# A transformer layer in float32: a second numerator buffer, the low planes' place and SyncE's order at steps 5 to 7

## What is computed

```
out = x + attention(xn) + ffn(xn)
attention: 16 heads of 16; Q, K, V = xn @ W.T + b; rotary embedding on Q and K;
           softmax(causal(Q K^T / 4)) V; concat @ Wo.T + bo
ffn:       h = relu(xn @ W_fc.T)^2;  y = h @ W_proj.T;
           5 steps of mem = 0.9 mem + y - [mem > 1], counting mem > 1; count / 5
```

## Time and profile before

| what | value |
|---|---|
| median of 3 runs | 2417.91 us (2417.7 to 2423.07) |
| the profiled execution | 2427.82 us |
| its span, first to last instruction | 2423.4 us |
| mean granted clock of TensorE | 0.965 |
| PE (TensorE matmul) busy | 2211.7 us, 91% |
| DVE (VectorE) busy | 1423.0 us, 59% |
| ACT (ScalarE) busy | 1436.5 us, 59% |
| POOL (GpSimd) busy | 1105.9 us, 46% |
| DMA | 297.45 MB, 123 GB/s |

### The profile page before, as it was taken

The page is one execution under the profiler, slowest core; times in us unless marked ns, Lnnn a source line. Parts: engine busy times, 40 slices in busy tenths (PEclk is TensorE's granted clock), DMA queues, the critical chain, the costliest instruction groups (busy, mean ns, idle before and its releaser), DMA issues.

```text
span 2423.4 us, 48395 instructions
## 1 busy us (share of the span) xinstructions
PE 2211.7 (91%) x16260; PEld 1410.4 (58%) x16260; DVE 1423.0 (59%) x2108; ACT 1436.5 (59%) x1669; POOL 1105.9 (46%) x1065
## 2 busy tenths in 40 slices
PE   3789999999998999999998999999999999999975
PEld 2656656566565656656565665656656565665632
DVE  5646665665656656565665656567565665666421
ACT  2175756656566565656656565566656656665662
POOL 2445454453544545354453545445354454544420
PEclk8899999999999999999999999999999999999987
DMA  3243453534545254453534445353454534444432
GB/s 126 93 126 107 118 160 87 166 94 117 150 108 163 83 142 130 114 166 87 161 96 125 141 117 156 84 170 110 116 151 101 163 88 136 136 123 142 106 97 55
DMA packets 167726, 297.45 MB, mean 123 GB/s; under 512 B 25009, under 2 KB 112817, under 8 KB 155057
## 3 DMA queue, kind: packets, MB, share of 16 engines
q1 hardware_dynamic: 167472, 294.01, 42.6%
HBM read 173.32 MB, written 102.76 MB: 114 GB/s over the span
## 4 chain that ended last, share of the span: by engine, by line
PE 62%; DVE 10%; issue 8%; DMA 7%; SPq 6%; ACT 5%; POOL 2%; DVEq 0%; ACTq 0%; POOLq 0%
PE pair L984 23%; PE pair L1171 14%; PE pair L1135 13%; PE pair L1154 10%; DMA qk_dram<-rot 6%; ACT probs L640 3%; SPq L343 3%; DVE rot L775 3%; SPq L388 1%; DVE count L857 1%; SPq L334 1%; DVE stats L722 1%; DVE rot L768 1%; PE pair L996 1%; POOL probs L553 1%
## 5 line engine op out<-in xcount | busy, mean ns | idle before, releaser
L640 ACT ACTIVATE probs<-pair 128x1024 f32<-128x1024 f32 x1152 | 1115.3, 1026 | 588.1 <-PE pair L1154 587.8
L1171 PE MATMUL pair<-probs,v_sb 128*17 128x512 f32 (+3 forms) x6144 | 584.9, 514 | 78.0 <-DVE numer L880 63.5
L553 POOL TENSOR_SCALAR_AFFINE_SELECT probs<-probs 128x512 f32<-128x512 f32 x512 | 396.0, 793 | 527.6 <-ACT probs L640 527.6
L545 POOL TENSOR_TENSOR h_lo<-h_sq,h_hi 128x512 fp32r<-128x512 f32 x256 | 385.4, 1506 | 469.7 <-DVE h_hi L843 469.2
L1154 PE MATMUL pair<-q_ring,k_ring 64*128 64x512 f32 (+3 forms) x3072 | 450.6, 386 | 48.7 <-ACT probs L640 26.1
L1154 PEld LDWEIGHTS pair<-q_ring,k_ring 64*128 64x128 f32 x3072 | 229.6, 187 | 328.2 <-ACT probs L640 170.3
L841 DVE TENSOR_TENSOR h_sq<-h_sq 128x512 f32<-128x512 f32 x256 | 189.0, 738 | 330.5 <-ACT h_sq L631 328.7
L1171 PEld LDWEIGHTS pair<-probs,v_sb 128*17 128x17 f32 x6144 | 155.0, 99 | 389.3 <-issue 282.6
L1135 PE MATMUL pair<-wproj_hi,h_hi 128*128 128x256 f32 x1024 | 293.3, 286 | 5.1 <-POOL h_lo L545 5.0
L631 ACT ACTIVATE h_sq<-pair 128x512 f32<-128x512 f32 x256 | 153.2, 598 | 238.7 <-PE pair L984 189.3
L857 DVE SCALAR_TENSOR_TENSOR count<-y_sb,count 128x512 bf16<-128x512 f32 x256 | 290.4, 1134 | 6.7
(11 more groups left out here) (87 smaller groups left out, 2587.9 us busy)
## 6 DMA issues: line engine op xcount, KB each, us to landing
q_ring<-qk_dram SPq DMA_DIRECT2D x384, 128.0 KB
k_ring<-qk_dram SPq DMA_DIRECT2D x384, 128.0 KB
qk_dram<-planes SPq DMA_DIRECT2D x64, 512.0 KB, 2.9
qk_dram<-rot SPq DMA_DIRECT2D x64, 512.0 KB, 3.7
xn<-in_x SPq DMA_DIRECT2D x16, 1024.0 KB, 8.5
rs<-in_x SPq DMA_DIRECT2D x64, 256.0 KB, 2.9
acc_dram<-rs SPq DMA_DIRECT2D x64, 256.0 KB, 4.4
attn<-numer SPq DMA_DIRECT2D x256, 64.0 KB, 2.3
```

The lines of the kernel that those rows point to most:

```text
L545: pool.tensor_tensor(h_lo[i % HB][:, :], h_sq[i % HB][:, :], h_hi[i % HB][:, :].bitcast(F32), ALU.subtract).then_inc(h_lo_done, 1)
L553: ins = pool.affine_select(view, view, [[0, 4], [1, P]], ALU.is_ge, 0.0, base=0, channel_multiplier=-1)
L640: act.activation(probs[BUFFER[n]][:, 2 * pr:2 * pr + 2, :], pair[m % NSLOT][:, :, :], ACT.Exp, scale=SCALE).then_inc(exp_done, 1)
L1171: ins = pe.matmul(pv_bank[32 * i:32 * i + VW, q0 - g * G:G], v_sb[:, kt, 4 * quad + i, :], probs[BUFFER[n]][:, i, at:at + width(kt, g)], s ...
```

## The change

`numer` becomes two buffers, used by quads in turn; only the first copies of quads 0 and 2 wait for gathers. The low planes are written to `rot_b` (the sum's second operand) instead of over `rot`, so `rotate` of units 2 and 3 waits for the low plane of units 0 and 1 ahead of L767, and for their store only ahead of L770. The h buffers are laid the other way round: h0, h1 over `rot`, h2, h3 over `rot_b`, and `rectify` 0 and 1 wait for `plane_lo`. On SyncE, `load_ring` of quad 2 comes ahead of `gather(b, 0)`, which moves to step 6, behind `store_planes` 2.

```diff
-        h_at = [rot_at + 4 * KB * n for n in (2, 3, 0, 1)]
+        h_at = [rot_at + 4 * KB * n for n in range(HB)]
...
-        numer = sb("numer", [P, S])
+        numer = [sb(f"numer{i}", [P, S]) for i in range(2)]
...
-                for lo, src in enumerate((planes[u % 2][:, :, :].bitcast(F32), rot[u % 2][:, :, :])):
+                for lo, src in enumerate((planes[u % 2][:, :, :].bitcast(F32), rot_b[u % 2][:, :, :])):
...
                     if att and n == 5:
-                        gather(b, 0, last)
                         load_ring(b, d, 2, b * 2 * NUNIT + 2 * NU)
                     if last and n in (6, 7):
                         store_out(b - 1, d - 1, n - 4)
-                    if more and n in (6, 7):
-                        store_planes(nb, nd, n - 4)
+                    if more and n == 6:
+                        store_planes(nb, nd, 2)
+                    if att and n == 6:
+                        gather(b, 0, last)
+                    if more and n == 7:
+                        store_planes(nb, nd, 3)
...
                 if i < 2:
-                    act.wait_ge(rot_sum, nb * 4 + 3 + i)
+                    act.wait_ge(plane_lo, nb * 4 + 3 + i)
...
                     if u >= 2:
-
-                        dve.wait_ge(planes_out[u % 2], (nb * 2 + 1) * 2 * 16)
+                        dve.wait_ge(plane_lo, nb * 4 + u - 1)
                     dve.scalar_tensor_tensor(part[:, 0, :], bank, bias, cos, ALU.add, ALU.mult)
                     dve.scalar_tensor_tensor(part[:, 1, :], bank, bias, sin, ALU.add, ALU.mult).then_inc(rot_even, 1)
                 else:
+                    if u >= 2:
+
+                        dve.wait_ge(planes_out[u % 2], (nb * 2 + 1) * 2 * 16)
                     dve.scalar_tensor_tensor(part_b[:, 0, :], bank, neg_bias, sin, ALU.subtract, ALU.mult, reverse0=True)
...
-                dve.tensor_tensor(rot[u % 2][:, :, :].bitcast(F32R), rot[u % 2][:, :, :], planes[u % 2][:, :, :].bitcast(F32), ALU.subtract
+                dve.tensor_tensor(rot_b[u % 2][:, :, :].bitcast(F32R), rot[u % 2][:, :, :], planes[u % 2][:, :, :].bitcast(F32), ALU.subtract
...
-                if g == 0 and (last or quad):
-
-                    if quad:
-                        dve.wait_ge(numer_in[(quad - 1) // 2], (b * 2 + (quad - 1) % 2 + 1) * 4 * 16)
-                    else:
-                        dve.wait_ge(numer_in[1], b * 2 * 4 * 16)
+                if g == 0 and quad % 2 == 0 and (last or quad):
+
+                    dve.wait_ge(numer_in[0 if quad else 1], (b * 2 + quad) * 4 * 16)
                     dve.wait_ge(denom_in, (b * NQUAD + quad) * 16)
-                dve.tensor_copy(numer[:, g * G:(g + 1) * G], pv_bank).then_inc(numer_done, 1)
+                dve.tensor_copy(numer[quad % 2][:, g * G:(g + 1) * G], pv_bank).then_inc(numer_done, 1)
```

More of the change, by code:

```diff
@@ L385, in gather @@
                 alone(sp, numer_done, (b * NQUAD + quad) * 2 + 2)
-                sp.dma_start(denom[base // 2:base // 2 + 32, :], numer[DK:P:32, :]).then_inc(denom_in, 16)
+                sp.dma_start(denom[base // 2:base // 2 + 32, :], numer[quad % 2][DK:P:32, :]).then_inc(denom_in, 16)
                 for i in range(4):
                     sp.dma_start(attn[base + DK * i:base + DK * (i + 1), k, :],
-                                 numer[32 * i:32 * i + DK, :]).then_inc(numer_in[k], 16)
+                                 numer[quad % 2][32 * i:32 * i + DK, :]).then_inc(numer_in[k], 16)
             def spread_recip(b, k, last):
```

## The result

The changed kernel takes 2353.03 us (median of 4 runs, 2348.59 to 2357.33) beside 2417.8 for the kernel before (median of 4). The ratio is 0.973, 95% interval 0.9705 to 0.9755. The forecast was 2340, in a range of 2320 to 2376. Of all executions behind this document one is left out: of the six of the kernel with SyncE's old order, one took 7726.51 us and the others 2391.92 to 2406.64.

What follows compares the result with a forecast made beforehand. TensorE's own work (busy 91%) was the floor, only its pauses to be had, chiefly the numerators' wait. 4.8 us in fifteen intervals (72) plus 6 made 78 us, off the median 2417.9: 2340 us, range 2320 to 2376.

Steps and rivals of the forecast that it cites:

- Numerators' wait: At step 7, TensorE's wait for the numerators' copy (63.5 us) falls under 6 us, slow clock gone: 5.7 us per interval.
- Low planes over `rot_b`: Units 2 and 3: odd halves end 1.3 and 2.65 us earlier; numerators' copy ends 1.4 us before TensorE needs it.
- ReLU's new wait for the low plane: First ReLUs wait for low planes of units 2 and 3; the added wait is covered with 1.3 us.
- Early even half: TensorE's wait for L768 before the last output product, about 7 us in all, ends; 6 us taken.
- What is late next: Step 8: TensorE waits about 1.4 us for GpSimd's masks instead of 0.51, costing 0.9 us per interval.
- The clock: Slow clock behind step 8's mask wait, charged one time in four: 0.4 us per interval.
- The sum: Per interval 5.7 + 0.4 - 0.9 - 0.4 = 4.8 us; fifteen times is 72, plus 6 for rotation waits: 78 us.
- SyncE's order: Moving ring ahead of gather costs nothing; ReLU 3's store wait goes, gaining 0.4 us per interval, bounds 0 and 0.6.
- the floor I named: Two numerator buffers alone gain 2.93 us of wait per interval at step 7; as a rival, 2374 us, chance 0.08.
- The ring: Rival: ring transfers right behind unit 1's store delay its landing; 8 us later gives 2446 us, chance 0.04.
- The copy did wait for the gather: Rival claimed the opposite: L880 waits for something else, such as the group before it in PSUM; 2415 us, chance 0.03.
- The mask rival: TensorE waits over 2 us for masks at step 8, clock falling each time; 3.1 us per interval, 2365, chance 0.2.

Runs made afterwards that it cites:

- the run with the late bias additions: The changed kernel with GpSimd's four bias additions of step 7 behind the masks instead of ahead of them: 2301.31 us, ratio 0.9503.

## Why the prediction was right, and where it was not

*Numerators' wait.* Right: 15 waits of about 4 us are gone with the slow clock behind them, and L882 has no idleness for a transfer. TensorE still waits 6.3 us for the copy in all, where under 6 was the sign. *Low planes over `rot_b`.* Right in mechanism. The copy was forecast to end 1.4 us before TensorE needs it; it had 0.84. The stop of the odd half was put at some 2 us and is 2.83 in unit 3. *ReLU's new wait for the low plane.* Covered, as said: no row of waits has it; the low plane of unit 2 ends at 1143.71 + 3.01 = 1146.72, 1.0 us before ReLU 0, where 1.3 was forecast. *Early even half.* The wait for the rotation in the intervals, about 7 us, is gone, and 3 us of the start-up's with it. The term of 6 us left out the slow clock behind such waits, though the earlier trace rows shows one: the planes alone gained 17 us.

*What is late next.* The place was right, the size was not: 2.51 us instead of 1.4. ReLU 0 started 1147.75 - 1147.44 = 0.3 us after the scores of unit 14, where I had it start with them; and the masks took 1.91 us, not the 1.22 of the earlier trace rows. VectorE's square of h1 fell beside them:

```profile
1154.47 0.67 DVE L846 TENSOR_TENSOR h_sq<-h_sq 128x512 f32<-128x512 f32 x1
```

In the run with the late bias additions, where it does not, the same two masks take 1.22. The difference of 0.69 us is about the square's 0.67; that the square is the cause is likely and was not tested by itself. The Trainium skill, SBUF — State Buffer, section Terms, says that VectorE and GpSimd share a port pair and that the loser is blocked for the whole instruction; the two durations agree with a shared port, without showing the blocking itself.

*The clock.* I charged one slow spell in four such pauses. Nine of 14 lowered it. The windows behind two pauses of equal length, granted clock in the third number from the end:

```profile
1156.40:1159.90 3.50, 3.43 (x26) 0.85 (x26) 2.62 (x3) 0.00 (x0) 1.42 (x2) 0.53 0.97 293
...
1437.30:1440.80 3.50, 3.47 (x32) 1.71 (x33) 2.60 (x3) 1.08 (x2) 1.40 (x1) 1.00 1.01 303
```

What sets the nine apart from the five was not found.

*The sum.* These two terms, 1.1 us of wait in 14 intervals and 5.5 slow spells of 1.55 us, made the forecast gain 24 us too large. The profiled executions, 2427.8 and 2352.5, nevertheless differ by 75 where 78 was the sum, so other terms were too small by about as much. The pages and wait lists say where. TensorE's waits for the numerators shrank by 57 us (63.5 to 6.3), for the rotation by 10 (14.9 to 4.8) and for the exponentials by 6 (26.1 to 20.2); its busy time fell by 27; the masks took 28 back (10.7 to 39.1). That makes 72 of the 75 us. The busy time is the surprise: fifteen spells of 1.55 us gone and nine back would be 9 us, not 27. The price of 1.55 us counted only the 16 instructions behind the wait, and in many intervals the slow clock lasted longer. TensorE in the kernel before, behind a wait of 4.41 us:

```profile
1331.21 3.61 PE L1171 MATMUL pair<-probs,v_sb 128*17 128x512 f32 x16 [4.41 <-DVE numer L880]
1334.75 1.22 PE L1154 MATMUL pair<-q_ring,k_ring 64*128 64x512 f32 x4
1335.90 1.64 PE L1068 MATMUL pair<-squares,sel 128*32 128x512 bf16 x8
```

At full speed the last two take 0.73 and 1.04 us. Over all 15 waits these spells come to some 30 us, an estimate from the same instructions' times at full speed, where the sum had 23. The rest is scattered, behind the rotation waits among other places, and is not assigned here. So the agreement of 75 with 78 is in part luck: two errors of some 20 us that cancel. The other 10 of the 13 us between the forecast and the median come from its base: the 78 us are a difference to an execution of 2427.8 us, and were taken off the median of 2417.9. The profiled execution of the changed kernel lies at its median (2352.5 and 2353.0), so the medians differ by 65 us.

*SyncE's order.* This step of the prediction failed: "I cost the move at nothing. It gives something", 0.4 us per interval. Without the move the other two parts give 0.9% instead of 2.7%. The forecast still came out since the move stood in the change for a gain of 0.4 us, and I had credited the 5.7 us to buffer and planes alone. That was luck. In truth buffer and order need each other: the buffer without the order gives nothing, the order with the planes and without the buffer loses 1.7%. The sign was in the earlier trace rows: ScalarE already waited 3.3 us per interval for the store (49.2 us in 15). I asked what this wait cost TensorE before, and not how long it would be once TensorE came 5 us earlier. For the same reason the floor I named, 2.93 us per interval from the buffer alone and 2374 us, was no floor: the buffer alone gave 0.2%, within noise.

*The rivals.* The ring did not hold up the store: landing was 3.9 us in the median against 3.7. The copy did wait for the gather: with two buffers its wait is gone. The mask rival described what happened better than the forecast did: over 2 us of wait each time, though the clock fell in nine of 14 and not in all. The result, 2353, lies midway between it (2365) and the forecast (2340).

## What to carry to other kernels

When a wait is removed, look for every chain that starts at the same release as the removed one and ends further on in the list of the engine that waited; here the last output product released the gather, and with it both the numerators' copy and, through an in-order queue, two stores. A wait of a side engine that costs nothing yet is a warning, and its length is not the slack: the slack is the time between a result and the main engine's need of it. ScalarE stood 3.3 us per interval for one store, and the store before it landed just as its ReLU began, with no slack for a TensorE that comes earlier. After each gain read the list of waits anew, since the next bound may be one line away: moving four additions behind two masks gave almost as much as the change itself, and gave nothing before it.

## What was not expected of the hardware

Pauses of 2.5 us of TensorE lowered the granted clock in nine of 14 cases, in intervals that run the same code, and the group of 24 behind them then took 3.2 to 3.6 us instead of 1.92. A pause of 1.19 us in the last interval was followed by a granted clock of 0.58 and a group of 3.32 us. A pair of masks on GpSimd took 1.91 us with VectorE's square beside it and 1.22 without. With 1.5 MB of ring transfers right behind it, a store landed about 0.3 us later: 3.96 us at most (1137.82 to 1141.78), where it was 3.69 at most in the kernel before (1173.58 to 1177.27).
